# Opening of the last stage: chunk 1's products, scores and norm among chunk 0's softmax and offsets

## What is computed

```
h = h + routed_ffn(layernorm(h))            # its rows come back by DMA: OG, gate
# last stage
q, k, v = split(layernorm(h) @ qkv_w.T + qkv_b);  q = q * SCALE     # 16 heads of 8
attn = softmax(q . k over a window of 7 positions + rpb)
h = h + (attn . v over the 7 positions) @ proj_w.T + proj_b
h = h + experts(layernorm(h))               # 6 dense experts; router weights per sequence
```

## Time and profile before

| | us |
|---|---|
| three runs | 812.06, 812.62, 812.61 (median 812.61) |
| profiled execution | 815.84 |
| its span | 814.0 |
| busy TensorE / VectorE / ScalarE / GpSimd | 621.3 / 630.1 / 531.2 / 286.9 |
| mean granted TensorE clock | 0.883 |

### The profile page before, as it was taken

The page is one execution under the profiler, slowest core; times in us unless marked ns, Lnnn a source line. Parts: engine busy times, 40 slices in busy tenths (PEclk is TensorE's granted clock), DMA queues, the critical chain, the costliest instruction groups (busy, mean ns, idle before and its releaser), DMA issues.

```text
span 814.0 us, 10976 instructions
## 1 busy us (share of the span) xinstructions
PE 621.3 (76%) x3142; PEld 478.3 (59%) x3143; DVE 630.1 (77%) x1275; ACT 531.2 (65%) x857; POOL 286.9 (35%) x313
## 2 busy tenths in 40 slices
PE   6997651836537291749779899978899999999997
PEld 3564551836537191747456789744667667667665
DVE  1687498999999999999688522156899999998953
ACT  1488899999999989984332434253586576575542
POOL 0465100000000000000158644344367677674642
PEclk9998886959687685959966799999999999999999
DMA  5372042355544444551611566220000000000000
GB/s 183 114 267 79 1 70 55 69 98 105 90 87 74 87 87 87 90 99 21 212 32 29 147 176 191 79 64 1 1 1 6 5 11 8 3 11 9 2 10 20
DMA packets 26386, 56.54 MB, mean 69 GB/s; under 512 B 4203, under 2 KB 15572, under 8 KB 25860
## 3 DMA queue, kind: packets, MB, share of 16 engines
q0 software_dynamic: 5728, 24.56, 16.0%
q1 hardware_dynamic: 19848, 30.80, 12.5%
q10 hardware_dynamic: 764, 0.62, 0.2%
HBM read 29.91 MB, written 10.17 MB: 49 GB/s over the span
## 4 chain that ended last, share of the span: by engine, by line
PE 36%; DVE 32%; issue 14%; ACT 11%; POOL 2%; DMA 2%; POOLq 1%; SPq 1%; DVEq 0%; ACTq 0%
DVE s_R L1296 4%; DVE s_R L1283 4%; PE psum L1834 4%; DVE s_R L1307 3%; DVE s_R L1756 3%; PE psum L2126 3%; PE psum L2051 2%; PE psum L2043 2%; PE psum L2113 2%; PE psum L1906 2%; PE psum L1907 2%; PE psum L1908 2%; DVE s_R L1288 2%; DVE s_R L1602 2%; PE psum L1997 1%
## 5 line engine op out<-in xcount | busy, mean ns | idle before, releaser
L1906 PE MATMUL psum<-s_xn_lo,s_split_hi 128*128 128x368 f32 x256 | 94.7, 370 | 137.5 <-ACT s_R L933 134.8
L1906 PEld LDWEIGHTS psum<-s_xn_lo,s_split_hi 128*128 128x128 f32 x256 | 54.7, 214 | 142.3 <-ACT s_R L933 137.6
L693 POOL DMA_DIRECT2D s_xnfm<-s_R x14 | 17.1, 1219 | 256.0 <-DVE s_R L1307 256.0
L1302 DVE TENSOR_TENSOR_SCAN s_R<-s_R 128x2944 f32<-128x2944 f32 x16 | 100.7, 6291 | 0.8
L1907 PE MATMUL psum<-s_xn_hi,s_split_lo 128*128 128x368 f32 x256 | 92.0, 359 | 0.0
L1908 PE MATMUL psum<-s_xn_hi,s_split_hi 128*128 128x368 f32 x256 | 91.5, 358 | 0.0
L1078 ACT ACTIVATE s_xnfm<-psum,s_cols 128x368 f32<-128x368 f32 x96 | 49.5, 565 | 55.2 <-PE psum L2115 55.2
L789 POOL TENSOR_TENSOR s_R<-s_R 128x368 f32<-128x368 f32 x48 | 50.7, 1056 | 47.4 <-DVE s_R L1756 45.7
L2126 PE MATMUL psum<-s_xnfm,s_R 128*128 128x368 f32 x192 | 66.1, 479 | 0.7 <-DVE s_R L1625 0.7
L940 ACT ACTIVATE s_R<-psum,s_cols 128x736 f32<-128x736 f32 x64 | 55.8, 876 | 14.0 <-PE psum L1908 9.5
L752 POOL TENSOR_TENSOR s_R<-s_R 128x368 f32<-128x368 f32 x47 | 45.8, 973 | 38.2 <-DVE s_R L1625 18.6
(11 more groups left out here) (264 smaller groups left out, 1642.4 us busy)
## 6 DMA issues: line engine op xcount, KB each, us to landing
s_xnfm<-s_R POOLq DMA_DIRECT2D x14, 1472.0 KB, 10.5
s_R<-in_w SPq DMA_DIRECT2D x28, 256.0 KB, 3.0
s_R<-in_xg SPq DMA_DIRECT2D x7, 744.0 KB, 4.2
x_sorted<-in_x_init SPq DMA_DIRECT2D x1, 5082.0 KB
s_wBC<-in_wBC SPq DMA_DIRECT2D x8, 256.0 KB, 2.7
s_R<-in_v SPq DMA_DIRECT2D x2, 1024.0 KB
s_R<-x_sorted SPq DMA_DIRECT2D x28, 66.0 KB, 2.5
s_R<-in_w SPq DMA_DIRECT2D x1, 1536.0 KB, 6.5
```

The costliest lines, as they stand in the source:

```text
L1302: dve.tensor_tensor_scan(bufB[:, u], ra[:, u], bufB[:, u], 0.0, ALU.mult, ALU.add).then_inc(ra_free, 1)
L1906: pe.matmul(bank(c), w_hi[:, s, u, k, :], xn_lo[:, a:b], start=True, stop=False)
```

## The change

- GpSimd doesn't drain at the end of the expert stage; it adds its 1 to `stage_done` and waits for 4.
- Trip 0 is written out on VectorE, TensorE and ScalarE, and the loops run from 1. On VectorE, `first_experts(1)` follows `first_experts(0)` and has its form (one instruction per sequence, no scaling by ScalarE); `first_experts(2)` stands between `shares(0)` and `shares_rest(0)`; `score_products(1)` follows chunk 0's offsets. `og_scaled` counts from chunk 2.
- The products of offsets 1 to 6 of chunk 0 go to six slots of `xnfm`, which nothing else uses yet (`product_slot`), so VectorE doesn't wait for GpSimd's additions there.
- On TensorE chunk 1's transposes and `qkv_of(1)` (banks 0, 1, 4) stand around `shares_fm(0)`, ahead of chunk 0's offsets; `project(0)` and `scores(1)` follow the offsets directly. `keep_busy(8)` of trip 0 becomes `keep_busy(6)`, and the single one behind `shares_fm(0)` goes. `project(0)` waits for all of chunk 0's offsets.
- On ScalarE `exponential(0)` comes before `normed_e(1)`; the Gelu table load after chunk 0 and the Exp load of chunk 1 go; `rows_scaled(1)` goes; `normed_e(2)` stands behind chunk 1's Gelu table load.
- On GpSimd `projection_bias(0)` stands behind `rstd_e(1)`, ahead of `weighted_sum(0)`.

```diff
--- before.py
+++ after.py
@@ -476,6 +476,15 @@
         wrt = take(NR, CB, NE)
         facc = take(CT)
         ftmp = take(3, CT)
+
+        def product_slot(c, o):
+            if o == 0:
+                return pv[:, c % 2]
+            return xnfm[:, o * CT:(o + 1) * CT] if c == 0 else pv_t[:, o % 2]
+
+        def qkv_banks(c):
+            return (0, 1, 4) if c == 1 else (6, 7, 3)
+
         fo = take(2, CB, D, parts=L)
         srep = take(CB)
         z = take(8, 16, parts=CB)
@@ -736,7 +745,8 @@
                                         ot[:, n % NSL], None).then_inc(ot_stored[n % NSL], 16)
             for s in range(NSL):
                 pool.wait_ge(ot_stored[s], 16 * (NTILE // NSL))
-            stage_end(pool, 4)
+            pool.sem_inc(stage_done, 1)
+            pool.wait_ge(stage_done, 4)
 
             def add_expert(f, e):
                 if not 0 <= f < NCH:
@@ -786,7 +796,7 @@
                     pool.wait_ge(pb_free, c * K + o + 1)
                     if o > 1:
                         pool.wait_ge(pv_add, c * (K - 1) + o - 1)
-                    pool.tensor_tensor(pv[:, c % 2], pv[:, c % 2], pv_t[:, o % 2], ALU.add).then_inc(pv_add, 1)
+                    pool.tensor_tensor(pv[:, c % 2], pv[:, c % 2], product_slot(c, o), ALU.add).then_inc(pv_add, 1)
                     if o == 2:
                         after_second()
 
@@ -795,10 +805,12 @@
             rstd_e(0)
             for c in range(NCH + 2):
                 add_expert(c - 3, NE)
-                if 1 <= c <= NCH:
+                if 2 <= c <= NCH:
                     projection_bias(c - 1)
                 if c + 1 < NCH:
                     rstd_e(c + 1)
+                if c == 0:
+                    projection_bias(0)
                 add_expert(c - 2, 1)
                 if 1 <= c <= NCH:
                     rstd_f(c - 1)
@@ -1053,7 +1065,6 @@
 
             normed_e(0)
             norm_copies(act, nE, 1, 0, (7, 7))
-            rows_scaled(1)
             act.sem_inc(nF.xT_free, 2)
             act.sem_inc(f_free, 2)
 
@@ -1088,7 +1099,7 @@
                 act.activation(ftmp[:, g % 3], bank((2, 4)[g % 2]), ACT.Copy).then_inc(fr_out, 1)
 
             def qkv_out(c):
-                for k, b in enumerate((6, 7, 3)):
+                for k, b in enumerate(qkv_banks(c)):
                     act.wait_ge(qkv_mm, c * 3 + k + 1)
                     act.activation(qkv[:, c % 2, k], bank(b), ACT.Identity,
                                    bias=qb if k == 0 else col("qkv_b", k),
@@ -1099,8 +1110,9 @@
                 act.activation(S_fm, bank(3, OH), ACT.Identity, bias=col("rpb_mid")[0:OH], scale=1.0).then_inc(S_ready, 1)
 
             def exponential(c):
-                load_table(ACT.Exp, 0)
-                if c + 1 < NCH:
+                if c != 1:
+                    load_table(ACT.Exp, 0)
+                if 2 <= c and c + 1 < NCH:
                     normed_e(c + 1)
                 act.wait_ge(sub_done, c + 1)
                 act.activation(P_tm[:, c % 2], P_tm[:, c % 2], ACT.Exp).then_inc(exp_done, 1)
@@ -1118,13 +1130,20 @@
                 act.wait_ge(PT_ready, c + 1)
                 act.activation(P_hi[:, c % 2], bank(3, OH), ACT.Copy).then_inc(P_hi_ready, 1)
 
-            for c in range(NCH + 2):
-                if c < NCH:
+            qkv_out(0)
+            act.wait_ge(wF_ready, 8 * 16)
+            act.activation(spread_r, spread, ACT.Copy).then_inc(spread_ready, 1)
+            act.activation(v1_hi[:, :, :], v1, ACT.Copy).then_inc(v1_hi_ready, 1)
+            rows_scaled(2)
+            scores_out(0)
+            exponential(0)
+            normed_e(1)
+            norm_copies(act, nE, 0, 1, (7, 7))
+            shares_out(0)
+            qkv_out(1)
+            for c in range(1, NCH + 2):
+                if 2 <= c < NCH:
                     qkv_out(c)
-                if c == 0:
-                    act.wait_ge(wF_ready, 8 * 16)
-                    act.activation(spread_r, spread, ACT.Copy).then_inc(spread_ready, 1)
-                    act.activation(v1_hi[:, :, :], v1, ACT.Copy).then_inc(v1_hi_ready, 1)
                 gelus(c - 2, 14, 16)
                 gelus(c - 2, 16, 18)
                 gelus(c - 2, 18, 20)
@@ -1132,12 +1151,14 @@
                     rows_scaled(c + 2)
                     scores_out(c)
                     exponential(c)
-                if 1 <= c <= NCH:
+                if c <= NCH:
                     normed_f(c - 1)
                     norm_copies(act, nF, (c - 1) % 2, c - 1, (5, 5), hi=xn_hi)
                 if c < NCH:
                     shares_out(c)
                     load_table(ACT.Gelu, 1)
+                if c == 1:
+                    normed_e(2)
                 if c >= NCH:
                     rest_out(c - 2)
                 gelus(c - 1, 0, 6)
@@ -1561,12 +1582,12 @@
 
             def first_experts(c):
 
-                if c:
-                    dve.wait_ge(og_scaled, c)
+                if c >= 2:
+                    dve.wait_ge(og_scaled, c - 1)
                     step.add(dve.tensor_tensor(seqs(H, c), seqs(OG, c), seqs(H, c), ALU.add))
                 else:
-                    dve.wait_ge(og_ready[0], 16)
-                    for j in range(CB):
+                    dve.wait_ge(og_ready[c], 16)
+                    for j in range(c * CB, (c + 1) * CB):
                         if j == 2:
                             dve.wait_ge(og_rest, 16)
                         step.add(dve.scalar_tensor_tensor(H[:, j, :], OG[:, j, :], gate[:, j:j + 1], H[:, j, :],
@@ -1749,15 +1770,25 @@
 
             def offset(c, o):
                 dve.wait_ge(pb_mm, c * K + o + 1)
-                if o >= 3:
+                if c and o >= 3:
                     dve.wait_ge(pv_add, c * (K - 1) + o - 2)
-                dst_t = pv[:, c % 2] if o == 0 else pv_t[:, o % 2]
-                for dst, a, b in windowed(c % 2, o, bank(6 + o % 2), 2, dst_t):
+                for dst, a, b in windowed(c % 2, o, bank(6 + o % 2), 2, product_slot(c, o)):
                     ins = dve.tensor_tensor(dst, a, b, ALU.mult)
                 ins.then_inc(pb_free, 1)
 
             first_experts(0)
-            for c in range(NCH + 2):
+            first_experts(1)
+            score_products(0)
+            dve.wait_ge(v1_hi_ready, 1)
+            dve.tensor_tensor(v1_lo[:, :, :], v1, v1_hi[:, :, :].bitcast(f32), ALU.subtract).then_inc(v1_split, 1)
+            scores_less_max(0)
+            shares(0)
+            first_experts(2)
+            shares_rest(0)
+            for o in range(K):
+                offset(0, o)
+            score_products(1)
+            for c in range(1, NCH + 2):
                 f, att = c - 1, c < NCH
                 tail = 0 <= f < NCH
                 if 0 <= f - 1:
@@ -1767,13 +1798,10 @@
                 if 0 <= f - 1 and not att:
                     weigh_rest(f - 1, 0)
                     weigh_rest(f - 1, 1)
-                if c + 1 < NCH:
+                if 2 <= c and c + 1 < NCH:
                     first_experts(c + 1)
-                if att:
+                if 2 <= c < NCH:
                     score_products(c)
-                if c == 0:
-                    dve.wait_ge(v1_hi_ready, 1)
-                    dve.tensor_tensor(v1_lo[:, :, :], v1, v1_hi[:, :, :].bitcast(f32), ALU.subtract).then_inc(v1_split, 1)
                 store_chunk(c - 3)
                 if tail:
                     residual_stats(f)
@@ -2153,16 +2181,16 @@
 
             def qkv_of(c):
                 pe.wait_ge(nE.xT_free, c + 3)
-                if c:
+                if c > 1:
                     pe.wait_ge(pb_free, c * K)
-                for k, b in enumerate((6, 7, 3)):
+                for k, b in enumerate(qkv_banks(c)):
                     pe.matmul(bank(b), w_qkv[:, k, :], fm(xfm, c), start=True, stop=True).then_inc(qkv_mm, 1)
 
             def project(c):
-                if c + 1 < NCH:
+                if c and c + 1 < NCH:
                     pe.wait_ge(qkv_ready, (c + 1) * 3 + 1)
                 else:
-                    pe.wait_ge(pb_free, NCH * K)
+                    pe.wait_ge(pb_free, (c + 1) * K)
                 pe.wait_ge(pv_add, (c + 1) * (K - 1))
                 for j in range(CB):
                     ins = pe.matmul(bank_tm(6)[:, j, :], pv[:, c % 2, j * L:(j + 1) * L], w_proj, start=True, stop=True)
@@ -2228,24 +2256,36 @@
                 pe.matmul(psum[:, 5, 464:464 + NE * CB], ones4, ewd.rearrange("p e b -> p (e b)"),
                           start=True, stop=True).then_inc(ew_mm, 1)
 
-            for c in range(NCH + 2):
+            qkv_of(0)
+            scores(0)
+            scores_tm(0)
+            keep_busy(6)
+            norm_transposes(pe, nE, 0, 1, (7, 7))
+            shares_fm(0)
+            qkv_of(1)
+            for o in range(K):
+                spread_out(0, o)
+                keep_busy(1, 2 * L)
+            project(0)
+            scores(1)
+            for c in range(1, NCH + 2):
```

(12 more changed lines are left out.)

## The result

| | before | changed |
|---|---|---|
| median, same chip (five runs each) | 812.62 us | 807.86 us |
| all runs | 812.06 to 815.55 | 805.25 to 809.42 |
| span of the profiled execution | 814.0 | 805.9 |
| ratio, 95% interval | | 0.9922, 0.9901 to 0.9944 |

The changed kernel is 4.8 us faster, where 5.2 were forecast (807.4). In a later comparison on one chip, with more runs, the ratio is 0.9935 (0.9911 to 0.9960).

The account below looks back on a forecast made before the run. No engine is full; the last stage's opening chain of waits was taken as the bound. offset(1, 0) starting 5.4 us earlier, less 0.2 behind it, gives 5.2: 812.6 - 5.2 = 807.4 us, range 806.2 to 810.9.

Parts of the forecast that it names:

- Drain to transposes: Last stage's opening: without the drain VectorE's updates end 2.2 us earlier, and with the clock kept up transposes start 3.1 earlier.
- Rival 4: Drain's time moves to GpSimd's next instruction, losing 2.2 to 3.1 us: 810.1, or about 812.6; chance 0.08.
- the sentence beside it: If the drain were a first-call code load of about 6 us, the drain at the kernel's end would be the first.
- Scores and exponential: Chunk 0: scores_out(0) 3.75 us earlier, exponential 5.5 earlier; first_experts(1) free inside VectorE's wait for q and k.
- The first offset: Start of offset(0, 0): 0.9 us lost to first_experts(2), gain 4.5 us, bounds 3.8 and 4.9.
- The meeting of additions and products: GpSimd's additions 4 to 6 against VectorE's score_products(1): end at 560.2 between products, or 563.2 if held.
- The likeliest case: Additions run between chunk 1's products, TensorE at the low clock: 807.4, range 806.9 to 808.6; chance 0.33.
- The clock: TensorE, idle 3.7 us before project(0), may fall to half rate for 3.5 us; scores end at 564.7 instead of 563.7.
- rival 5: TensorE stays at the low level through the following chain, 8.4 us of work doubled: 817.0, slower than before; chance 0.05.
- Rival 2: Additions between products with TensorE at the high clock: 6.2 us off, 806.4; chance 0.20.
- Behind it: After offset(1, 0): normed_e(2) before the first gelu delays gelus 0.86 us; counted as 0.2 lost, between 0 and 0.9.
- Rival 6: Steady loop takes the gain back through GpSimd or TensorE running late: within 0.2% of 812.6; chance 0.04.

Follow-up runs that it names:

- experiments 1 and 2: Drain put back into the changed kernel (30.07 us from first OG load's issue to offset(0, 0)); only the drain removed from the kernel before (28.79 us).
- experiment 3: Kernel before with an extra GpSimd drain behind its first memset; 54.6 us from first OG load's issue to offset(1, 0).
- experiment 4: Kernel before with an extra GpSimd drain between its 32 indirect DMAs into x_sorted and the expert stage's 28; 52.74 us to offset(1, 0).
- experiment 5: Changed kernel with normed_e(1) again ahead of chunk 0's exponential on ScalarE; 49.94 us from first OG load's issue to offset(1, 0).
- experiment 9: Changed kernel with GpSimd's fourth addition of chunk 0 also waiting for VectorE's first product of chunk 1; 49.84 us to offset(1, 0).
- experiment 7: Changed kernel with six filler matmuls (3.85 us) ahead of project(0) on TensorE; 47.0 us from first OG load's issue to offset(1, 0).
- experiment 10: Changed kernel run again without edit; 809.78 us against 814.78 for the kernel before, ratio 0.9935; 50.74 us to offset(1, 0).
- experiment 1: Changed kernel with GpSimd's drain put back at the expert stage's end; 51.53 us from first OG load's issue to offset(1, 0).

## Why the prediction was right, and where not

*Drain to transposes.* The first update came 3.87 us after the mark (4.1 forecast, 6.41 before) and the transposes 10.35 (10.45 forecast): 3.2 gained where 3.1 stood, and experiments 1 and 2 give 3.17 for it at the first offset. The 1.1 us that the fillers held the transposes were the clock, as argued: 5.80 us for 18.

*Where the drain's time goes.* Rival 4 was wrong in its place: nothing moved to the next instruction, and the memset ran at 522.65, in its usual 0.09. But the sentence beside it was half right. The time did go to the drain at the kernel's end; only not since it was the first drain. The Trainium skill's figure of about 6 us for a first call (GPSIMD Engine Reference, "Instruction dispatch") met 6.1 us here by chance: experiment 3 has a first drain of 0.04 us, and in experiment 4 the drain's length went with the count of DMAs. No run here shows a load of code.

*Scores and exponential.* `scores_out(0)` came 17.89 us after the mark, 18.15 forecast. The exponential: 20.73, 21.0 forecast. The reordering was credited with 1.8 us; experiment 5 gives the order 0.9 and leaves the other half to the moved `first_experts(1)`, which the prediction had put at nothing. It was one step early in its accounting: an instruction that was free where it stood had also taken `rstd_e(1)` out of VectorE's products.

*The first offset.* Gain 5.06, forecast 4.5 with bounds of 3.8 and 4.9: just outside, and so, by the prediction's own sign, wrong in this step, on the better side. The mis-sized term is the 0.9 us for `first_experts(2)`. From the end of the shares to the offset it took 3.1 us, not 3.4, and there VectorE's queue and `qkv_of(1)` on TensorE end within 0.15 us of one another. The other 0.25 is the sum of the small ones above.

*The meeting of additions and products.* The likeliest case took place. The chain of waits of the changed kernel (start, us, what) shows additions 4 to 6 in a row among the products, 1.10 to 1.19 apart:

```profile
553.46 0.97 POOL s_R L799
...
554.56 1.06 POOL s_R L799
...
555.75 1.05 POOL s_R L799
```

They ended at 556.8, 34.9 us after the mark (35.6 forecast), and VectorE paid instead: 5.36 us for its products. The first three of them waited for one addition each and stood 1.2 us apart; the additions kept their pace (3.35 us for the three ahead of the products, 3.33 for the three among them). That is the alternation by instruction which the Trainium skill's exclusive port gives (SBUF — State Buffer, "SBUF: two separate sides"), with the trace's numbers beside it. The 3.24 us rows don't fit that rule, and experiment 9 removed my reason for keeping them apart (from a wait, or from work). The forecast took the right row, for a reason that isn't the right one. It also read that row a little wrong: VectorE's first product there lasted 0.85 us in all, where such a one usually lasts 0.23, so it was held for 0.6.

*The clock.* The forecast had it low for 3.5 us of work and priced that at 1.0 against the high level. Experiment 7 gives 2.2. This term was mis-sized, and by two halves. At the low level the scores ended 13.15 us after `offset(0, 0)`, where 12.65 were forecast, because the level lasted 5.1 us from the start of `project(0)` and not 3.5. At the high level they would have ended 0.65 earlier than forecast (11.0 in experiment 7, not 11.65), because VectorE's last product came 10.1 us after the offset and not 10.8; the scores then ended 0.9 after it, as forecast. In experiment 10 the low level lasted over 10 us. That is the mechanism of rival 5, which had a chance of 0.05 and was priced with everything doubled. It came true in part, in one of two executions of the same program. Rival 2 rested on a fall that came more than 4 us after TensorE's last work; here the fall came about 2.2 us after it (last filler to 552.95, mean 0.58 in 555 to 556). So the old row gave no bound.

Two errors cancelled, and that the sum met its mark is luck: the first offset was 0.55 us better than forecast, the stretch behind it 0.5 us worse (22.15 against 21.65). There is a slip in the sum as well: 579.19 - 573.7 is a gain of 5.5, not 5.4.

*Behind it.* +0.2 us, as forecast, in the profile of the changed kernel, and within 0.6 in all others. `normed_e(2)` ahead of the gelus stayed under VectorE's own work. Rival 6 is out.

*In sum:* 49.05 us from the mark to `offset(1, 0)` in the profile (49.1 forecast), 5.55 less than before, and 4.8 in the medians. The medians lie a little below what the profile gives; the low level's changing length, 1.7 us between two executions, is of that size.

## What to carry to other kernels

Price a moved step by its mark in the stage, not by the span: here 2.7 of the 8.1 us by which two spans differed came from stages that nobody touched. When an engine is freed from one wait (seven slots, 0.6 us), look at what it runs into next and at who goes idle meanwhile: TensorE's new wait of 4 us cost 1.5 to 3.9 us through its clock, more than the slots brought, and 3.85 us of filler matmuls won it back. A single profile can't size such a step, since one program gave two prices 1.7 us apart. A drain behind many GpSimd DMAs is worth moving to a place where nobody waits for it; here that one line is more than half of the gain.

## What the runs showed of the hardware

- A GpSimd drain lasted about 0.083 us for each DMA that GpSimd has issued since its last one (6.12 us for 74, 2.34 for 28, 0.04 for none; one drain behind 46 of them fits worse, 4.4 us), even over 270 us after the last of them (the last drain of the changed kernel). Ordinary instructions don't pay for them (the memset behind them took 0.09 us).
- Two-operand SBUF instructions of VectorE and GpSimd's additions alternated one by one: 1.2 us for a product that takes 0.43 alone, 1.1 for an addition, as without the products. A tiny `tensor_scalar` of GpSimd that met such a run of products was held for all of it, 3.24 us, in each profile. Open.
- Around a wait of 4.0 us and the same work behind it, TensorE's low level lasted about 3.4, 6.8 and 10.2 us in three executions (experiment 1, the changed kernel, experiment 10; estimates from the windows' means), the last two of the same program. In experiment 4 the clock fell with no wait over 1.5 us in the 8 us ahead of it (1.00 in 551 to 552, 0.56 in 552 to 553).
